# ScalarE issues the first loads of W, SyncE those of x, beta and the bias: a blocked matrix product with a fast multiplication scheme

## The chip, the cores and the metric

The kernel runs on one core of a Trainium2 chip. Times are device microseconds of one execution. PE is TensorE's matmul, PEld its weight load, DVE is VectorE, ACT is ScalarE, POOL is GpSimd, SP is SyncE, and SPq the instructions with which SyncE hands a transfer to the DMA engines. "L377" is line 377 of the kernel.

## The reference

```
B, N, H, L = (2048, 512, 1024, 8)          # rows of x, inner, outputs, factors
s = jnp.einsum('bn,hln->bhl', x, beta)
ssq = jnp.einsum('bn,hln->bhl', x * x, beta * beta)
fm = 0.5 * jnp.sum(s * s - ssq, axis=-1)
linear_out = x @ W.T + b
return fm + linear_out
```

Everything is float32: x is 2048 x 512, beta 1024 x 8 x 512, W 1024 x 512.

## The kernel before

All three parts are products of x (2048 x 512) with a right operand of 512 rows. They are done in passes over the right operand, each with 1024 columns: pass 0 multiplies by W, passes 1 to 8 by an eighth of beta each (the products are then squared and summed over the 8 factors), and a last pass multiplies the squares of x by the summed squares of beta. Within a pass the kernel goes over 8 pairs of row tiles of x (256 rows). A "group" `g` is one pair in one pass, 80 in all.

Each group is a 2 x 2 block product. The blocks of x are A11, A12, A21, A22 and those of the right operand B11, B12, B21, B22. From the third group on a scheme with seven products in place of eight is used, which needs sums of blocks (S1 to S4, T1 to T4). The first two groups (`DIRECT = 2`) use the blocks as they are, since their sums aren't there yet. Every float32 operand is split into a high part that the array takes exactly (`*_hi`, a cast) and the rest (`*_lo`, a subtraction), and each product is three matmuls of 128x128 by 128x512: high x high, high x low, low x high. The casts of the opening are ScalarE's (one is VectorE's), the subtractions VectorE's. For B12 of W alone the high part stands in a slot of `t_lo` (`t_lo[:, 1, T2]`) and the low part in the one beside it.

The order on each engine is written out by hand, and engines meet through semaphores. In the opening TensorE does this:
- nine warm-up matmuls on constants (L461), which wait for no load;
- `first_parts` (L486 to L503), 24 matmuls: x of pair 0, then of pair 1, times B11. It has two halves of the inner dimension (k = 0, 1). For pair 0 each half comes with its half of B11 in one load, `first_p[k]` (tile `first`, which lies in `cs`);
- the products of both pairs with B12 (L509 to L513), 24 matmuls, which appear as L468, L472 and L474 on `t_lo`;
- the products with B21 and B22 (L515 to L520), and then the groups of seven products.

ScalarE waits for `first_p[0]`, then `first_p[1]`, x of pair 1 (L674, L675), B12 (L676, L677), the rest of x of pairs 0 and 1 (L679), B21 and B22, and casts each as it comes. Nothing else is ahead of its first wait but the load of its function table. VectorE follows with the low parts.

All loads are issued by SyncE, in the order of its code:

```
sp.dma_start(first[:, k, 0:2 * P + COLS], first_p[k])      # L377, k = 0 and 1
sp.dma_start(... x_p[1][:, 0:2 * KP * P])                  # L378, x of pair 1
load_first(B12, b12_loaded)                                # L278
sp.dma_start(... x_p[0:DIRECT, :, 2 * KP * P:] ...)        # L381, the rest of x of pairs 0 and 1
sp.wait_ge(first_loaded[KP - 1], 16)
load_first(B21, b21_loaded); load_first(B22, b22_loaded)   # L278
```

and then x of pairs 2 and 3 (L287), the first beta blocks (L282, L283) and the bias (L390). SyncE next waits for TensorE's first products. The loads have these sizes: `first_p` 2 x 384 KB with rows of 3 KB, x of pair 1 256 KB with rows of 2 KB, each block of W 512 KB with rows of 4 KB, the rest of x of pairs 0 and 1 512 KB.

Of the kernel before, what the change touches and what calls it, by code (L numbers as in the profile page):

```python
# [12 lines left out]
KP = 2  # L13
# [13 lines left out]
T1, B22, B11, B21, T2, T3, T4 = range(OPS)  # L27
B12 = T1
# [89 lines left out]
def fm_layer(nc, first_p, x_p, beta_p, w_p, bias, out):  # L118
# [12 lines left out]
    with ExitStack() as ctx:  # L131
# [3 lines left out]
        def sem(name):  # L135
            return ctx.enter_context(nc.semaphore(name))


        with ExitStack() as early:
            def early_sb(name, shape):  # L140
                return early.enter_context(nc.sbuf_tensor(name, shape, f32))

            t_hi_in = early_sb("t_hi_in", [P, 2, OPS, KP, COLS])
# [22 lines left out]
        first_loaded = [sem(f"first_loaded{k}") for k in range(KP)]  # L166
# [3 lines left out]
        b21_loaded = sem("b21_loaded")  # L170
        b12_loaded = sem("b12_loaded")
        b22_loaded = sem("b22_loaded")
# [80 lines left out]
        def t_at(n, op):  # L253

            return t_hi_in[:, 1, op, :, :] if n == 0 else t_lo_in[:, n % 2, op, :, :]
# [17 lines left out]

        @block.sync
        def _(sp):
            def load_first(op, loaded):

                sp.dma_start(t_hi_in[:, 1, op, :, :], w_p[op]).then_inc(loaded, 16)  # L278

            def load_blocks(n):  # L280
                source = q_kept.rearrange("p a b k h -> p (a b) k h") if n == Q_PASS else beta_p[n - 1]
                sp.dma_start(t_lo_in[:, n % 2, 0:2, :, :], source[:, 0:2, :, :]).then_inc(right_loaded, 16)  # L282
                sp.dma_start(t_lo_in[:, n % 2, 2:4, :, :], source[:, 2:4, :, :]).then_inc(left_loaded, 16)  # L283

            def load_x(g):
                blocks = x_at(g)[:, 0:4, :].rearrange("p b c -> p (b c)")
                sp.dma_start(blocks, x_p[pair_of(g)]).then_inc(x_loaded[slot_of(g)], 16)  # L287
# [88 lines left out]
            for k in range(KP):  # L376
                sp.dma_start(first[:, k, 0:2 * P + COLS], first_p[k]).then_inc(first_loaded[k], 16)  # L377
            sp.dma_start(s_lo_in[:, 1, 0:2, :].rearrange("p b c -> p (b c)"), x_p[1][:, 0:2 * KP * P]  # L378
                         ).then_inc(x_second_loaded, 16)
            load_first(B12, b12_loaded)  # L380
            sp.dma_start(s_lo_in[:, 0:DIRECT, 2:4, :].rearrange("p g b c -> p g (b c)"),  # L381
                         x_p[0:DIRECT, :, 2 * KP * P:].rearrange("g p c -> p g c")).then_inc(x_rest_loaded, 16)

            sp.wait_ge(first_loaded[KP - 1], 16)
            load_first(B21, b21_loaded)
            load_first(B22, b22_loaded)
            load_x(2)
            load_x(3)
            load_blocks(1)
# [175 lines left out]
        def _(act):  # L565
# [53 lines left out]
            def split_first_x(k):  # L619
                nc.scalar.copy(s_hi[:, 0, 0:2, k * P:(k + 1) * P], first_x(k)).then_inc(s_hi_ready, 1)  # L620
# [40 lines left out]
            def square_rest(g):  # L661
# [4 lines left out]
                nc.scalar.activation(squares_at(g)[:, COLS:], squares_at(g)[:, COLS:], ACT.Square  # L666
                                     ).then_inc(squared, 1)

            act.wait_ge(first_loaded[0], 16)
            split_first_x(0)  # L670
            act.wait_ge(first_loaded[1], 16)
# [430 lines left out]
```

## Time and profile before

| what | value |
|---|---|
| median of three runs | 775.32 us (775.0 to 775.35) |
| the profiled execution | 775.58 us |
| its span | 773.6 us |
| PE busy | 769.4 us of the span |
| DVE, ACT, POOL busy | 575.0, 395.3, 328.3 us |
| first warm-up matmul, first real matmul | 0.78 us, 4.39 us |

The span runs from the first instruction that the profile shows to the last. Busy times count instructions that compute, so an engine that waits or hands out a transfer isn't busy. A bracket behind a row of the timeline says how long the engine sat idle ahead of it and what ended that.

### The profile page before, as it was taken

The numbers are of one execution on the slowest core, as the hardware profiler recorded it, in microseconds if no ns is written. First come the engines' busy times: TensorE is split into PE (matmuls) and PEld (weight loads), VectorE is DVE, ScalarE is ACT, GpSimd is POOL, SyncE is SP. The second block draws the span as 40 slices with busy tenths as digits, with TensorE's granted clock in tenths as the row PEclk, the third lists the DMA queues.
The fourth block names the chain that finished last, engine by engine and source line by source line (L and its number), as shares of the span: only waits on it lengthen the run. The fifth ranks groups of instructions, "written<-read, shape, count | busy, mean of one in ns | idle before, by whom it ended". The sixth has DMA issues, their size and how long they took to land.

```text
span 773.6 us, 9628 instructions
## 1 busy us (share of the span) xinstructions
PE 769.4 (99%) x3381; PEld 633.5 (82%) x3381; DVE 575.0 (74%) x595; ACT 395.3 (51%) x503; POOL 328.3 (42%) x252
## 2 busy tenths in 40 slices
PE   9999999999999999999999999999999999999998
PEld 6888888888888888888888888888888888888886
DVE  6999289958765876587658765876587658788986
ACT  4674356645554555455545554555455545553430
POOL 0243274345434643454345434543454357334111
PEclk9999999999999999999999999999999999999999
DMA  8697853286604660466046604650565056629843
GB/s 339 262 363 320 311 192 116 79 287 214 222 28 150 217 218 28 149 218 218 28 150 221 221 28 155 218 212 28 169 226 197 28 186 206 224 75 387 337 163 123
DMA packets 64288, 145.34 MB, mean 188 GB/s; under 512 B 4848, under 2 KB 41712, under 8 KB 61936
## 3 DMA queue, kind: packets, MB, share of 16 engines
q1 hardware_dynamic: 64240, 144.72, 52.4%
q8 instruction: 27, 0.44, 0.2%
q14 instruction: 21, 0.17, 0.1%
HBM read 102.76 MB, written 41.94 MB: 187 GB/s over the span
## 4 chain that ended last, share of the span: by engine, by line
PE 98%; DMA 1%; ACT 0%; DVE 0%; SPq 0%; issue 0%
PE bank L472 33%; PE bank L474 33%; PE bank L468 33%; DMA t_hi_in<-w_p 1%; DVE t_lo L889 0%; ACT t_lo L677 0%; SPq L377 0%; ACT cs L725 0%; SPq L378 0%
## 5 line engine op out<-in xcount | busy, mean ns | idle before, releaser
L472 PE MATMUL bank<-t_lo,s_hi 128*128 128x512 f32 x1116 | 434.2, 389 | 0.2 <-DVE t_lo L889 0.2
L468 PE MATMUL bank<-t_hi,s_hi 128*128 128x512 f32 x1108 | 431.1, 389 | 0.0
L474 PE MATMUL bank<-t_hi,s_lo 128*128 128x512 f32 x1108 | 431.0, 389 | 0.0
L472 PEld LDWEIGHTS bank<-t_lo,s_hi 128*128 128x128 f32 x1116 | 209.5, 188 | 44.0 <-DVE t_lo L889 0.6
L468 PEld LDWEIGHTS bank<-t_hi,s_hi 128*128 128x128 f32 x1108 | 208.0, 188 | 43.4 <-ACT r L650 0.3
L474 PEld LDWEIGHTS bank<-t_hi,s_lo 128*128 128x128 f32 x1108 | 208.0, 188 | 43.2
L863 DVE TENSOR_REDUCE sums<-cs 128x256 f32<-128x2048 f32 x64 | 146.3, 2285 | 120.8 <-issue 86.4
L1035 POOL TENSOR_TENSOR r<-r 128x512 f32<-128x512 f32 x70 | 94.8, 1355 | 257.5 <-ACT r L650 257.5
L1039 POOL TENSOR_TENSOR cs<-r 128x512 f32<-128x512 f32 x70 | 94.0, 1343 | 121.6 <-issue 119.9
L658 ACT ACTIVATE cs<-bank 128x512 f32<-128x512 f32 x64 | 38.3, 598 | 204.4 <-PE bank L474 204.4
L731 DVE TENSOR_TENSOR t_lo<-t_lo_in,t_hi 128x1024 fp32r<-128x1024 f32 x63 | 108.2, 1721 | 0.0
L666 ACT ACTIVATE cs<-cs 128x1536 f32<-128x1536 f32 x64 | 95.5, 1493 | 0.0
L1008 POOL TENSOR_TENSOR t_lo_in<-t_lo_in 128x1024 f32<-128x1024 f32 x32 | 78.9, 2465 | 0.1
L854 DVE TENSOR_TENSOR cs<-bank,r 128x512 f32<-128x512 f32 x70 | 48.3, 690 | 33.8 <-PE bank L474 33.8
L567 ACT CAST t_hi<-t_lo_in 128x1024 fp32r<-128x1024 f32 x63 | 65.6, 1046 | 4.0 <-DVE t_lo_in L746 4.0
L644 ACT COPY r<-bank 128x512 f32<-128x512 f32 x71 | 41.8, 588 | 49.5 <-PE bank L474 47.2
L638 ACT COPY r<-bank 128x512 f32<-128x512 f32 x78 | 46.1, 591 | 34.6 <-PE bank L474 34.6
L842 DVE TENSOR_TENSOR r<-bank,r 128x512 f32<-128x512 f32 x78 | 53.4, 684 | 10.5 <-PE bank L474 10.2
L617 ACT CAST s_hi<-s_lo_in 128x1792 fp32r<-128x1792 f32 x16 | 27.2, 1701 | 56.4 <-DVE s_lo_in L812 56.3
L848 DVE TENSOR_TENSOR cs<-bank,r 128x512 f32<-128x512 f32 x70 | 48.4, 691 | 7.6 <-PE bank L474 1.8
L1046 POOL TENSOR_TENSOR acc<-acc,bias_all 128x256 f32<-128x256 f32 x64 | 49.0, 766 | 4.2 <-DMA acc<-acc_kept 4.2
L650 ACT COPY r<-bank 128x512 f32<-128x512 f32 x71 | 41.0, 578 | 2.8 <-PE bank L474 2.8
(77 smaller groups left out, 304.2 us busy)
## 6 DMA issues: line engine op xcount, KB each, us to landing
s_hi<-s_hi_kept SPq DMA_DIRECT2D x30, 896.0 KB, 5.1
s_lo<-s_lo_kept SPq DMA_DIRECT2D x30, 896.0 KB, 7.1
t_lo_in<-beta_p SPq DMA_DIRECT2D x16, 1024.0 KB, 7.1
s_lo_in<-x_p SPq DMA_DIRECT2D x17, 512.0 KB, 6.3
acc_kept<-cs SPq DMA_DIRECT2D x16, 512.0 KB, 5.0
acc<-acc_kept SPq DMA_DIRECT2D x64, 128.0 KB, 5.4
acc_kept<-acc SPq DMA_DIRECT2D x64, 128.0 KB, 1.8
s_hi_kept<-s_hi SPq DMA_DIRECT2D x8, 896.0 KB, 6.3
```

Source lines behind the costliest of these rows:

```text
L468: nc.tensor.matmul(to, s_hi[:, slot, s_op, cols], hi[:, k, :], start=start, stop=False, skip_group_check=True)
L472: nc.tensor.matmul(to, s_hi[:, slot, s_op, cols], lo[:, k, :], start=False, stop=False, skip_group_check=True)
L474: return nc.tensor.matmul(to, s_lo[:, slot, s_op, cols], hi[:, k, :], start=False, stop=stop, skip_group_check=True)
L567: nc.scalar.copy(t_hi[:, n % 2, op, :, :], t_at(n, op)).then_inc(t_hi_ready, 1)
L666: nc.scalar.activation(squares_at(g)[:, COLS:], squares_at(g)[:, COLS:], ACT.Square).then_inc(squared, 1)
L731: nc.vector.tensor_tensor(t_lo[:, n % 2, op, :, :], t_at(n, op), as_f32(t_hi[:, n % 2, op, :, :]), ALU.subtract).then_inc(t_lo_ready, 1)
L842: nc.vector.tensor_tensor(r2[:, :], bank(g, BANK_B), r1[:, :], ALU.add).then_inc(r2_added, 1)
L863: nc.vector.tensor_reduce(sums[:, :, :].rearrange("p r h -> p (r h)"), squares_at(g).rearrange("p (h l) -> p h l", l=L), AX_X, ALU.add).th ...
L1008: nc.gpsimd.tensor_tensor(t_at(n, op), t_at(n, left), t_at(n, right), ALU.subtract).then_inc(t_summed, 1)
L1035: nc.gpsimd.tensor_tensor(r5[:, :], r5[:, :], r7[:, :], ALU.add).then_inc(r57_added, 1)
L1039: nc.gpsimd.tensor_tensor(cs[:, g % 2, 1, 1, :], r5[:, :], r2[:, :], ALU.add).then_inc(c22_added, 1)
L1046: nc.gpsimd.tensor_tensor(acc[:, g % 2, :, :], acc[:, g % 2, :, :], part, ALU.add).then_inc(acc_biased, 1)
```

## The change

ScalarE hands out the three loads of W ahead of its first wait, and SyncE no longer does. SyncE's wait for the second piece of `first_p` goes with them. SyncE's other loads keep their order, the destination and size of every load are the same, and so are all semaphores that ScalarE and VectorE wait for.

```diff
--- before.py
+++ after.py
@@ -273,10 +273,6 @@
 
         @block.sync
         def _(sp):
-            def load_first(op, loaded):
-
-                sp.dma_start(t_hi_in[:, 1, op, :, :], w_p[op]).then_inc(loaded, 16)
-
             def load_blocks(n):
                 source = q_kept.rearrange("p a b k h -> p (a b) k h") if n == Q_PASS else beta_p[n - 1]
                 sp.dma_start(t_lo_in[:, n % 2, 0:2, :, :], source[:, 0:2, :, :]).then_inc(right_loaded, 16)
@@ -377,13 +373,8 @@
                 sp.dma_start(first[:, k, 0:2 * P + COLS], first_p[k]).then_inc(first_loaded[k], 16)
             sp.dma_start(s_lo_in[:, 1, 0:2, :].rearrange("p b c -> p (b c)"), x_p[1][:, 0:2 * KP * P]
                          ).then_inc(x_second_loaded, 16)
-            load_first(B12, b12_loaded)
             sp.dma_start(s_lo_in[:, 0:DIRECT, 2:4, :].rearrange("p g b c -> p g (b c)"),
                          x_p[0:DIRECT, :, 2 * KP * P:].rearrange("g p c -> p g c")).then_inc(x_rest_loaded, 16)
-
-            sp.wait_ge(first_loaded[KP - 1], 16)
-            load_first(B21, b21_loaded)
-            load_first(B22, b22_loaded)
             load_x(2)
             load_x(3)
             load_blocks(1)
@@ -666,6 +657,13 @@
                 nc.scalar.activation(squares_at(g)[:, COLS:], squares_at(g)[:, COLS:], ACT.Square
                                      ).then_inc(squared, 1)
 
+            def load_w(op, loaded):
+
+                nc.scalar.dma_start(t_at(0, op), w_p[op]).then_inc(loaded, 16)
+
+            load_w(B12, b12_loaded)
+            load_w(B21, b21_loaded)
+            load_w(B22, b22_loaded)
             act.wait_ge(first_loaded[0], 16)
             split_first_x(0)
             act.wait_ge(first_loaded[1], 16)
```

On SyncE, the beginning of its program; the names are destination<-source, `cs` holds `first`, `t_hi_in` the blocks of W. Before:

```order
L377 DMA cs<-first_p 128x768 x2
L378 DMA s_lo_in<-x_p 128x512
L278 DMA t_hi_in<-w_p 128x1024
L381 DMA s_lo_in<-x_p 128x2x512
L278 DMA t_hi_in<-w_p 128x1024 x2
L287 DMA s_lo_in<-x_p 128x1024 x2
```

On SyncE now:

```order
L373 DMA cs<-first_p 128x768 x2
L374 DMA s_lo_in<-x_p 128x512
L376 DMA s_lo_in<-x_p 128x2x512
L283 DMA s_lo_in<-x_p 128x1024 x2
L278 DMA t_lo_in<-beta_p 128x2048
```

The three loads of W are gone, and the loads of x and beta follow each other.

On ScalarE, the beginning of its program, before:

```order
L620 ACT_TABLE_LOAD
L620 CAST s_hi<-cs 128x2x128 x2
L673 CAST t_hi<-cs 128x512
L675 CAST s_hi<-s_lo_in 128x512
L677 CAST t_lo<-t_hi_in 128x1024
```

On ScalarE now:

```order
L662 DMA t_hi_in<-w_p 128x1024 x3
L611 ACT_TABLE_LOAD
L611 CAST s_hi<-cs 128x2x128 x2
L671 CAST t_hi<-cs 128x512
L673 CAST s_hi<-s_lo_in 128x512
L675 CAST t_lo<-t_hi_in 128x1024
```

The three loads stand ahead of the table load; everything behind them keeps its order.

## Rows read from the trace of the kernel before

**Rows 1.** The page: span, busy time by engine, and the chain that ended last.

```profile
span 773.6 us, 9628 instructions
...
PE 769.4 (99%) x3381; PEld 633.5 (82%) x3381; DVE 575.0 (74%) x595; ACT 395.3 (51%) x503; POOL 328.3 (42%) x252
...
PE 98%; DMA 1%; ACT 0%; DVE 0%; SPq 0%; issue 0%
```

**Rows 2.** The stretch after the opening: start:end, length, each engine's busy us.

```profile
24.00:770.00 746.00, 746.00 (x3292) 617.48 (x3291) 558.21 (x575) 380.84 (x486) 328.06 (x248) 1.00 0.52 185
```

**Rows 3.** End of the chain: start us, us, what.

```profile
770.32 0.24 PE bank L474
```

**Rows 4.** Timeline from 0 to 20 us: start, us, engine, line, operation, count, [idle before].

```profile
0.73 1.28 ACT L620 ACT_TABLE_LOAD   x1 [0.73 <-PEq L1095]
0.74 0.86 SPq L377 DMA_DIRECT2D cs<-first_p  x2
...
0.78 3.82 PE L461 MATMUL bank<-const-bfloat16-1.0 128*128 128x512 bf16 x9 [0.78 <-PEq L1095]
...
2.12 0.43 SPq L278 DMA_DIRECT2D t_hi_in<-w_p  x1
...
3.81 0.41 ACT L620 CAST s_hi<-cs 128x256 fp32r<-128x256 f32 x1 [1.80 <-DMA cs<-first_p]
...
4.39 0.69 PE L494 MATMUL bank<-t_hi,s_hi 128*128 128x512 f32 x2
...
4.79 0.41 ACT L620 CAST s_hi<-cs 128x256 fp32r<-128x256 f32 x1 [0.57 <-DMA cs<-first_p]
...
5.86 1.52 SPq L287 DMA_DIRECT2D s_lo_in<-x_p  x2
5.91 0.67 PE L494 MATMUL bank<-t_hi,s_hi 128*128 128x512 f32 x2
...
7.08 0.62 ACT L675 CAST s_hi<-s_lo_in 128x512 fp32r<-128x512 f32 x1 [1.35 <-DMA s_lo_in<-x_p]
...
7.75 0.73 PE L494 MATMUL bank<-t_hi,s_hi 128*128 128x512 f32 x2 [0.26 <-ACT s_hi L675]
...
9.06 1.05 ACT L677 CAST t_lo<-t_hi_in 128x1024 fp32r<-128x1024 f32 x1 [1.36 <-DMA t_hi_in<-w_p]
...
10.14 1.22 DVE L889 TENSOR_TENSOR t_lo<-t_hi_in,t_lo 128x1024 fp32r<-128x1024 f32 x1 [1.72 <-ACT t_lo L677]
...
10.88 0.39 PE L468 MATMUL bank<-t_lo,s_hi 128*128 128x512 f32 x1
...
11.42 0.50 PE L472 MATMUL bank<-t_lo,s_hi 128*128 128x512 f32 x1 [0.15 <-DVE t_lo L889]
...
11.99 0.39 PE L468 MATMUL bank<-t_lo,s_hi 128*128 128x512 f32 x1
...
16.54 0.39 PE L474 MATMUL bank<-t_lo,s_lo 128*128 128x512 f32 x1
...
19.82 0.42 DVE L805 TENSOR_TENSOR s_lo_in<-s_lo_in 128x256 f32<-128x256 f32 x1
```

**Rows 5.** The first load of `first_p` alone: its issue, and its time to landing.

```profile
L377 SPq DMA_DIRECT2D cs<-first_p x1: 388/388/388, 0.7 to 0.7; - x1
...
DMA to landing us min/median/max: 3.1/3.1/3.1
```

**Rows 6.** Stretches of the opening; last columns: PEclk, DMA share, GB/s.

```profile
0.00:3.00 3.00, 2.23 (x6) 0.86 (x7) 0.00 (x0) 1.28 (x1) 0.20 (x4) 1.00 0.41 119
3.00:4.00 1.00, 1.00 (x4) 0.31 (x3) 0.18 (x1) 0.18 (x1) 0.00 (x0) 1.00 1.05 397
5.00:6.00 1.00, 1.00 (x6) 0.57 (x5) 0.90 (x3) 0.72 (x2) 0.00 (x0) 1.00 0.37 92
8.00:9.00 1.00, 1.00 (x4) 0.53 (x4) 0.42 (x1) 0.00 (x0) 0.00 (x0) 1.00 1.07 422
```

**Rows 7.** The page's DMA queues: packets, MB, share.

```profile
q1 hardware_dynamic: 64240, 144.72, 52.4%
```

## The prediction

> **What bounds the kernel now.** I read the page first: PE is busy 769.4 of a span of 773.6 us, and the chain that ended last is 98% PE [rows 1]. The reader is to see that nothing but PE's start, its holes and its end can move the time. Then the stretches: from 24 to 770 us PE has no hole at all, 746.00 busy of 746.00 us [rows 2], and its last matmul begins at 770.32 [rows 3]. What is left is the opening, read from the timeline of the first 17 us [rows 4].
>
> The reader is to see there how thin the opening's slack is. The nine warm-up matmuls on constants take 3.82 us from 0.78, to 4.60. The first piece of `first_p` lands 3.1 us after its issue at 0.74 [rows 5], and ScalarE's first cast starts at 3.81. The first real matmul follows at 4.39, when the warm-up is all but over. Matmuls that wait for nothing go at one every (16.54 - 11.99) / 20 = 0.2275 us. The 24 matmuls of `first_parts` run from 4.39 to 10.88, that is 6.49 us where 24 x 0.2275 = 5.46 would do: 1.03 us lost, partly before the second half of `first_p` is cast and most of it at 7.75, behind x of pair 1. The first product with B12 waits again: its second matmul starts at 11.42, where 10.88 + 0.23 = 11.11 was due, 0.31 us for `t_lo` of B12. So all that earlier loads could give back in the whole kernel is 1.03 + 0.31 = 1.34 us, and the B12 product, had its first matmul been followed without a gap, in effect starts at 11.19.
>
> The profiled execution took 775.58 us, 0.26 over the median of 775.32; the sums below are differences, added to 775.58 and then lowered by 0.26. 0.2% of this kernel is 1.55 us: about what its measurement can tell from no change. All of the 1.34 us is less than that.
>
> **The change, part by part.**
>
> *ScalarE issues three loads ahead of its first work.* No row shows ScalarE issuing a load. SyncE's issues take 0.43 us each at the start, and 1.52 / 2 = 0.76 with a long queue [rows 4]. Three of them put the table load, which starts at 0.73 now, at 2.02 (with 0.43) or 3.01 (with 0.76), and its 1.28 us end at 3.30 or 4.29. I take 0.43, as an empty queue is what SyncE has at that time too: 3.30 is before the cast at 3.81, so this costs nothing; the load of `first_p` hides it. The other end, 4.29, would delay the first cast by 0.48 us if `first_p` still landed at 3.81, and nothing if it lands as late as I expect below.
> The Trainium skill (ScalarE: Activation LUTs, "What ACT_TABLE_LOAD costs" and the table-load gate before it) puts a table load at about 2.7 us; by that it would end at an estimated 4.7. This case's row has 1.28 us, and the row decides.
>
> *SyncE no longer issues B12, B21, B22 and has no wait.* It loses one issue of 0.43 ahead of the rest of x for pairs 0 and 1, and its wait for the second piece of `first_p`, which landed at 4.79. So x of pairs 2 and 3, beta and the bias are issued some 3.3 us earlier (x of pair 2 at about 2.6 for 5.86). All of them stand behind the rest of x in SyncE's own order, none is wanted before 19 us (the first use of x of pair 2 is the sum at 19.82 [rows 4]), and they can't pass what PE waits for in the opening. Gain and cost on the path: nothing.
>
> *W's 1.57 MB now compete with `first_p`.* This is the term that decides. Before, one queue served loads in the order of their issue: `first_p` (2 x 0.393 MB), x of pair 1 (0.262 MB), and B12 only then. Now B12, B21 and B22 are offered at the same time as `first_p`, from another queue. No row shows two queues of loads side by side: the page has one, q1 [rows 7], beside two for instructions. So the cost is bounded. From below: W gets only what `first_p` leaves, and costs nothing. From above: each of the two queues gets a turn, row by row, and W's rows are 4 KB against 3 KB of `first_p` and 2 KB of x of pair 1. Between them lie equal shares by bytes. In the rows of a stretch each [rows 6] the DMA engines move 119 GB/s over the first three us and 397 in the fourth, so 0.356 MB by 3.0 and 0.753 MB by 4.0, and I let it go on at 400 (422 is seen between 8 and 9). The engines' share is already 1.05 in 3 to 4 us: nothing is free there for a second queue, what it gets is taken.
>
> Now 0.393 MB are moved by 3.1 and land at 3.81, so landing comes 0.7 us after the bytes. Shares by bytes: the first piece needs 0.786 MB, moved at 4.1, landed at 4.8; the second 1.57 MB, 6.05, landed 6.75; x of pair 1 2.10 MB, 7.4, landed 8.1. Shares by rows: 0.918 MB, landed 5.1; 1.835 MB, landed 7.4; 2.62 MB (with which W is through), landed 9.4.
> PE follows. From the first landing it is 4.39 - 3.81 = 0.58 to the first matmul, from the second 5.91 - 4.79 = 1.12, from that of x of pair 1 7.75 - 7.08 = 0.67 [rows 4].
> - By bytes: first matmul 5.4, its six end 6.75; the next six wait for 6.75 + 1.12 = 7.87 and end 9.23; x of pair 1 is ready at 8.77; twelve more end at 9.23 + 2.73 = 11.96. Against 11.19: **+0.77 us**.
> - By rows: 5.7, then 7.4 + 1.12 = 8.52, ending 9.89; x of pair 1 ready at 10.07; twelve more end at 12.80. Against 11.19: **+1.6 us**.
> I take the middle, +1.2 us, as the row length does differ but nothing shows that turns go by rows.
>
> The Trainium skill speaks against the change too (DMA: Bandwidth & Descriptors, "Queues, rings and completion order", and "Issuing engines are not separate DMA queues"): loads of ScalarE and SyncE run on the same 16 DMA engines, which take turns between the queues by packet, and a second issuer only saves issue time. Its turns would give the sum between the two above; the trace of before, with one queue, can't confirm it.
>
> *B12 comes earlier.* In either reckoning B12 lands before x of pair 1, so ScalarE's cast of it (1.05 us, right behind the 0.62 us one of x of pair 1) and VectorE's 1.22 us no longer end after PE wants them: by rows 9.4 + 0.62 + 1.05 + 1.22 = 12.3, with PE there at 12.8. The 0.31 us wait and the 0.26 us hole at 7.5 go; both are inside the sums already, since PE is charged from landings. What is late next is the second piece of `first_p`.
>
> *Sum:* issues 0, SyncE 0, sharing and PE's new waits +1.2: 775.58 + 1.2 = 776.8 profiled, less 0.26 is **776.5**.
>
> **The rivals.**
> - *W does not hold up `first_p`; the waits go (other side).* Place: the landing at 3.81. Should W's rows start behind `first_p` by a us or so, or should the slow stretch at 5 to 6 us (92 GB/s, share 0.37 [rows 6]), when B12 was issued and yet little moved, be filled by the other queue, PE would start at 4.39 as now and lose less than 1.34 us. For it: that trough, over 1 us of engines all but idle with loads queued. Against: the share of 1.05 at 3 to 4. It decides if the first piece lands before about 4.2. Time: 775.32 - 1.34 = 774.0 at best, 774.9 with a third of it. Chance 0.20. A page of the Trainium skill (Perfetto Trace Analysis, its list on DMA) has the same hope: balancing over issuers may help where descriptor generation bounds. The trough could be that; nothing here shows it.
> - *PE falls back to its low clock.* Warm-up matmuls go at 3.82 / 9 = 0.42 us each, 512 columns at 1.2 GHz, later ones at 0.2275, as they only can at 2.4. The page's granted clock is 1.00 in all stretches, so it is the spacing that tells. PE would now stand from 4.60 to 5.4 or 5.7, and again for 1.1 to 1.5 us before the second piece; no hole of before is longer than 0.3. If one more stretch like the warm-up ran at the low level, nine matmuls at 0.42 for 0.23 cost 1.8 us more: 776.5 + 1.8 = 778.3. Decides if the first real matmuls are some 0.43 apart. Chance 0.10, with slow first rows of W (a queue's first packets blocking both) in the same figure.
> - *The forecast's own case,* shares of either kind: 0.70, its own range 775.7 to 777.3.
>
> **How the numbers follow.** 776.5 is the likeliest case. The range reaches down to 774.8, into the first rival, and up to 778.0, short of the second: it leaves out perhaps 0.07 below and 0.09 above. Slower by over 1.55 us (above 776.87): all of the clock rival, 0.10, and a third of the forecast's case (shares by rows, +1.6, is just there), 0.25: 0.35. Faster by over 1.55 us needs more than the waits hold; 0.02 for what I don't see. Within: 0.63.
>
> **What would show it.** The first cast of ScalarE at 4.8 to 5.1 for 3.81; the second cast of x of pair 0 at 6.7 to 7.4 for 4.79; first real matmul at 5.4 to 5.7; the three W loads landed before 9.5, B22 above all; the wait on VectorE's `t_lo` at the first B12 product gone; no hole in PE after 13 us; GB/s near 400 already at 3 to 6 us. It is wrong if `first_p` lands by 4.2 (then W does not compete, and the time is at or below 775.3), if it lands after 6 (W gets more than its turn), if matmuls behind the first wait are 0.43 apart, or if PE shows a hole later, which I excluded.

## The result

Median 777.63 us (777.51 to 778.08, 7 runs) against 775.32 us (774.88 to 775.38, 7 runs): the ratio is 1.0032, 95% interval 1.0023 to 1.0042. The change costs 2.3 us. The range, 774.8 to 778.0, holds the time; the forecast of 776.5 named the way but half of the size.

The page of the changed kernel, its span, busy times and chain:

```profile
span 775.7 us, 9628 instructions
...
PE 769.2 (99%) x3381; PEld 633.6 (82%) x3381; DVE 574.7 (74%) x595; ACT 395.6 (51%) x503; POOL 328.7 (42%) x252
...
PE 98%; DMA 1%; ACT 0%; SPq 0%; issue 0%
```

PE's work is the same (769.2 us for 769.4), and the span is 2.1 us longer. In the chain beside PE stands a load of `first_p` now, where the kernel before had the load of B12. From 24 to 770 us nothing changed, and the last matmul is late by 772.38 - 770.32 = 2.06 us [rows 3]:

```profile
24.00:770.00 746.00, 746.00 (x3292) 617.48 (x3292) 557.48 (x575) 382.17 (x487) 327.79 (x248) 1.00 0.52 184
```

```profile
772.38 0.24 PE bank L465
```

So the loss is in the opening, whose timeline (all engines) reads:

```profile
0.73 1.38 ACTq L662 DMA_DIRECT2D t_hi_in<-w_p  x3
...
0.77 3.62 PE L452 MATMUL bank<-const-bfloat16-1.0 128*128 128x512 bf16 x9 [0.77 <-PEq L1093]
...
2.14 1.28 ACT L611 ACT_TABLE_LOAD   x1 [2.14 <-issue]
...
5.55 0.41 ACT L611 CAST s_hi<-cs 128x256 fp32r<-128x256 f32 x1 [2.13 <-DMA cs<-first_p]
...
6.12 0.70 PE L485 MATMUL bank<-t_hi,s_hi 128*128 128x512 f32 x2 [1.73 <-DVE t_hi L878]
...
7.65 0.40 ACT L611 CAST s_hi<-cs 128x256 fp32r<-128x256 f32 x1 [1.70 <-DMA cs<-first_p]
...
8.72 0.70 PE L485 MATMUL bank<-t_hi,s_hi 128*128 128x512 f32 x2 [0.92 <-ACT t_hi L671]
...
9.62 0.62 ACT L673 CAST s_hi<-s_lo_in 128x512 fp32r<-128x512 f32 x1 [1.04 <-DMA s_lo_in<-x_p]
...
10.29 0.73 PE L485 MATMUL bank<-t_hi,s_hi 128*128 128x512 f32 x2
...
11.02 0.73 PE L489 MATMUL bank<-t_hi,s_lo 128*128 128x512 f32 x2
11.22 1.22 DVE L887 TENSOR_TENSOR t_lo<-t_hi_in,t_lo 128x1024 fp32r<-128x1024 f32 x1 [0.26 <-ACT t_lo L675]
...
13.40 0.39 PE L459 MATMUL bank<-t_lo,s_hi 128*128 128x512 f32 x1
...
13.63 0.39 PE L463 MATMUL bank<-t_lo,s_hi 128*128 128x512 f32 x1
```

Against [rows 4]: the first cast at 5.55 for 3.81, the second at 7.65 for 4.79, that of x of pair 1 at 9.62 for 7.08. PE is idle from 4.39 to 6.12 and from some 7.8 to 8.72. The B12 product starts at 13.40 and runs on without a gap. The prediction puts its start before at 11.19 in effect, from its second matmul. But the third was late too: the fourth began at 11.99 [rows 4], so the start was in effect at 11.99 - 3 x 0.2275 = 11.31. The loss is 13.40 - 11.31 = 2.09 us, which agrees with the 2.06 of the last matmul. ScalarE's table load ends at 3.42, long before the first piece lands.

Three stretches of [rows 6] again (last columns: PEclk, DMA share, GB/s), and what each queue moved from 3 to 5 us; q10 is ScalarE's, q1 SyncE's. The columns are packets, MB and share of the DMA engines; a packet is a row here, but for a few of 4 bytes that end a load:

```profile
0.00:3.00 3.00, 2.23 (x6) 0.87 (x7) 0.00 (x0) 0.86 (x1) 0.20 (x4) 1.00 0.40 67
3.00:4.00 1.00, 1.00 (x4) 0.30 (x3) 0.00 (x0) 0.42 (x1) 0.00 (x0) 1.00 0.96 335
5.00:6.00 1.00, 0.00 (x0) 0.00 (x0) 0.44 (x2) 0.41 (x1) 0.00 (x0) 1.00 1.01 408
```

```profile
q10 hardware_dynamic: 111, 0.42, 58.7%
q1 hardware_dynamic: 113, 0.32, 40.2%
```

In this stretch the queues take turns row by row: 111 of W against 113 of `first_p`, and so 0.42 MB against 0.32. The start is slower too, 67 GB/s over three us for 119, while the trough at 5 to 6 us is gone (408 GB/s for 92).

### The profile page after: what moved, and what is told of

Same layout as the page of the kernel before. It is cut to its first block, busy times and chain, and to the rows that moved or that the text cites. A ratio compares the mean times of both kernels' runs of the same rounds, so it can differ in the third digit from the quotient of the medians.

```text
span 775.7 us, 9628 instructions
## 1 busy us (share of the span) xinstructions
PE 769.2 (99%) x3381; PEld 633.6 (82%) x3381; DVE 574.7 (74%) x595; ACT 395.6 (51%) x503; POOL 328.7 (42%) x252
## 4 chain that ended last, share of the span: by engine, by line
PE 98%; DMA 1%; ACT 0%; SPq 0%; issue 0%
PE bank L459 33%; PE bank L465 33%; PE bank L463 33%; DMA cs<-first_p 1%; PE bank L485 0%; PE bank L489 0%; PE bank L493 0%; ACT cs L723 0%; ACT t_hi L671 0%; ACT s_hi L611 0%; SPq L373 0%
```

## The experiments

My theory after the result: two queues take turns, so W's bytes hold up `first_p`, and the whole loss is that. Its rivals: SyncE's missing wait crowds the opening; ScalarE's issues and its late table load cost; W is dear from ScalarE wherever it is issued; PE's clock falls in its idle time. Times are medians of 11 runs where not said otherwise, beside runs of the kernel before on the same chip (775.40 us for the first four, 775.23 for the next, 775.24 for the last), and the ratios with their 95% intervals. Every "spare" load goes to memory that nothing uses until 19.8 us. Each kernel has one profiled execution. Those of tiny_first (776.02 us), tiny_b12 (775.41), act_late (783.04) and touch_late_b12 (776.35) are the slowest runs of their kernels, so their rows tell less of the medians.

| run | us | ratio |
|---|---|---|
| hold_off | 775.41 | 1.0000 (0.9991 to 1.0008) |
| act_b12 | 776.15 | 1.0016 (1.0007 to 1.0025) |
| spare_4k (6 runs) | 777.83 | 1.0030 (1.0019 to 1.0042) |
| spare_tiny | 774.93 | 0.9991 (0.9982 to 1.0000) |
| spare_1k | 777.04 | 1.0022 (1.0013 to 1.0031) |
| tiny_first | 775.31 | 0.9999 (0.9990 to 1.0008) |
| tiny_b12 | 775.07 | 0.9997 (0.9988 to 1.0006) |
| act_late (4 runs) | 782.00 | 1.0089 (1.0075 to 1.0103) |
| touch_late | 775.07 | 0.9997 (0.9988 to 1.0006) |
| touch_late_b12 | 775.11 | 0.9998 (0.9989 to 1.0007) |
| act_b12_warm | 776.08 | 1.0011 (1.0002 to 1.0020) |
| touch_sp | 776.20 | 1.0011 (1.0002 to 1.0020) |

**hold_off: the SyncE part alone.**

```diff
-            sp.wait_ge(first_loaded[KP - 1], 16)
             load_first(B21, b21_loaded)
```

> The kernel before without SyncE's wait for the second piece of first_p; SyncE still issues all loads, W's in their old places. Theory of the queues (two queues take turns, so W's bytes delay first_p): nothing competes here, first cast at 3.8 us, second cast at 4.8, time 775.3, within 0.3. Theory of SyncE (the loads of x 2 and 3, beta and the bias, no longer held back, are what crowds the opening): the whole loss of 2.3 us is here, 777.6, with the first cast at 5.5.

No change in the time; first cast at 3.81, second at 5.01 (4.8 was expected). SyncE's earlier loads aren't the loss.

**act_b12: a third of the bytes.**

```diff
-            load_first(B12, b12_loaded)          # SyncE
+            nc.scalar.dma_start(t_at(0, B12), w_p[B12]).then_inc(b12_loaded, 16)   # ahead of ScalarE's first wait
```

> ScalarE issues B12 alone ahead of its first wait, 0.52 MB in place of 1.57; SyncE issues B21 and B22 where it did, behind its wait. Theory of the queues: the first piece of first_p still lands near 5.5 us, since both queues are full that long, but the second comes 0.52 MB / 400 GB/s = 1.3 us earlier than in the changed kernel, at 6.3 for 7.65; PE then runs through from the first landing and loses 0.4 us on before: 775.7. Theory of the order of W (it is B21 and B22 that hurt): first_p back at 3.8 and 4.8, and B12's wait gone, 775.0. Theory of a fixed price for a second queue: as the changed kernel, 777.6.

Timeline of ScalarE and PE:

```profile
5.29 0.41 ACT L619 CAST s_hi<-cs 128x256 fp32r<-128x256 f32 x1 [2.84 <-DMA cs<-first_p]
...
5.87 0.70 PE L493 MATMUL bank<-t_hi,s_hi 128*128 128x512 f32 x2 [1.10 <-DVE t_hi L880]
...
6.41 0.41 ACT L619 CAST s_hi<-cs 128x256 fp32r<-128x256 f32 x1 [0.72 <-DMA cs<-first_p]
...
11.67 0.39 PE L467 MATMUL bank<-t_lo,s_hi 128*128 128x512 f32 x1
```

The second piece is cast at 6.41, where 6.3 was expected; the first is as late as with three loads (5.29). The B12 product starts at 11.67, +0.36 us on 11.31, and the profiled execution is 0.35 us longer than that of before. The median, 775.40 + 0.75, is above the 775.7 that was expected, for the 11 runs fell into two groups, six from 775.93 to 776.15 and five from 777.31 to 777.71; the profile is of the lower (775.93), which is what the theory foresaw. act_b12_warm below takes that up.

**spare_4k: the bytes alone.** SyncE's program is the one before, every load of W in its old place.

```diff
+            for i, op in enumerate((B12, B21, B22)):      # ScalarE, ahead of its first wait
+                nc.scalar.dma_start(spare[i], w_p[op].rearrange("p k c -> p (k c)")).then_inc(spare_loaded[i], 16)
```

> The kernel before, with SyncE as it was, and three more loads of 0.52 MB by ScalarE ahead of its first wait, with rows of 4 KB (the same three blocks of W) to memory that is still unused. Theory of the queues: first_p lands as in the changed kernel, first cast 5.55, second 7.65; B12 comes through SyncE after 3.1 MB at about 10.7, its low part at about 13.0, just in time for PE at 13.4: 777.6. Theory that it was taking W from SyncE's order that cost: 775.3, first cast at 3.8.

```profile
5.46 0.40 ACT L621 CAST s_hi<-cs 128x256 fp32r<-128x256 f32 x1 [2.04 <-DMA cs<-first_p]
7.57 0.40 ACT L621 CAST s_hi<-cs 128x256 fp32r<-128x256 f32 x1 [1.71 <-DMA cs<-first_p]
```

The whole loss is back, with both casts within 0.1 us of the changed kernel's, although W came through SyncE as before. It is the competing bytes, not who issues the W that is used.

**spare_tiny: the issues without the bytes.**

```diff
+                nc.scalar.dma_start(spare[i][:, 0:16], w_p[op][:, 0, 0:16]).then_inc(spare_loaded[i], 16)
```

> As before, with three loads by ScalarE ahead of its first wait that move 64 bytes in each of 128 rows of B12, B21 and B22 to unused memory: the issues and the late table load, without the bytes. Theory of the queues: first cast at 3.8 to 3.9, time within 0.3 of 775.3. Theory of the issues (ScalarE's three issues and the table load behind them are the loss): first cast late by 1 us or more, 776.5 or above. A third possibility: the slow stretch of DMA at 5 to 6 us is the first touch of W by every DMA engine; touched early, B12 lands before 8.7 for 9.0 and the 0.31 us wait goes: 775.0.

ScalarE's timeline, PE's, and the stretch from 5 to 6 us:

```profile
2.14 1.28 ACT L621 ACT_TABLE_LOAD   x1 [2.14 <-issue]
...
4.12 0.41 ACT L621 CAST s_hi<-cs 128x256 fp32r<-128x256 f32 x1 [0.69 <-DMA cs<-first_p]
...
4.69 1.19 PE L495 MATMUL bank<-t_hi,s_hi 128*128 128x512 f32 x2
...
5.68 0.96 PE L499 MATMUL bank<-t_hi,s_lo 128*128 128x512 f32 x2
...
6.32 0.62 ACT L680 CAST s_hi<-s_lo_in 128x512 fp32r<-128x512 f32 x1
...
6.94 0.61 PE L495 MATMUL bank<-t_hi,s_hi 128*128 128x512 f32 x2
...
8.32 1.05 ACT L682 CAST t_lo<-t_hi_in 128x1024 fp32r<-128x1024 f32 x1 [1.37 <-DMA t_hi_in<-w_p]
```

```profile
2.00:3.00 1.00, 1.00 (x4) 0.43 (x3) 0.00 (x0) 0.86 (x1) 0.00 (x0) 1.00 0.57 190
5.00:6.00 1.00, 1.00 (x3) 0.81 (x3) 0.76 (x2) 0.62 (x2) 0.00 (x0) 1.00 0.97 315
```

Three issues and the table load at 2.14 cost nothing: the first cast waited for its load, not for the table. The signs of the third possibility came: 315 GB/s in the trough for 92, x of pair 1 cast at 6.32 for 7.08, B12 at 8.32 for 9.06. The price is the first piece, 4.12 for 3.81, since the third us is slower (190 GB/s). By its median this is the fastest kernel here, 0.47 us under before, with an interval that ends at 1.0000.

**spare_1k: turns by rows, or shares by bytes.** As spare_4k, to memory in rows of 1 KB (the end of the line is left out):

```diff
+                nc.scalar.dma_start(s_lo_in[:, 0:4, S1 + i, :], w_p[op].rearrange("p k (r c) -> p (k r) c", c=256)
```

> As spare_4k, the same 1.57 MB of W a second time ahead of ScalarE's first wait, but to memory in rows of 1 KB. If the two queues take turns row by row, first_p with its 3 KB rows gets 3/4 of the rate for 3/7: second cast at 5.9 to 6.2 for 7.57 in spare_4k, PE at the end of first_parts at 11.2 for 13.3, time 775.4. If they share by bytes, the second cast stays near 7.2 to 7.6 and the time at 777 or above.

The second cast came at 6.26 us for 7.57, next to the 5.9 to 6.2 of turns by rows. The time didn't follow (777.04): B12 was cast only at 10.28, and PE, at the B12 product by 12.08, waited for its low part. The queues from 3 to 5 us:

```profile
q10 hardware_dynamic: 347, 0.36, 52.2%
q1 hardware_dynamic: 138, 0.37, 47.8%
```

Bytes are about even here, 0.36 against 0.37 MB, and rows aren't: 347 to 138. So this run is against strict turns by rows as well. ScalarE's issues with split rows also took 2.13 us for 1.38, and its queue moved nothing before 3 us, which let the first piece go ahead: VectorE casts from it at 3.96. ScalarE's cast is at 4.19, for here its table load ran from 2.90 to 4.18, the one trace in which it was in the way, by some 0.2 us. The run is inconclusive on the rule; it shows only that short rows hold `first_p` up less.

**tiny_first and tiny_b12: which touch fills the trough.** The same small loads, from `first_p` (the end of the line is left out), and from B12 alone:

```diff
+                nc.scalar.dma_start(spare[i][:, 0:16], first_p[i % 2][:, 256 * (i // 2):256 * (i // 2) + 16]
---
+            nc.scalar.dma_start(spare[0][:, 0:16], w_p[B12][:, 0, 0:16]).then_inc(spare_loaded[0], 16)
```

> As spare_tiny, but the three loads of 64 bytes a row read first_p in place of B12, B21 and B22. If the trough of DMA at 5 to 6 us is the first touch of W, it is back: under 150 GB/s there for 315 in spare_tiny, x of pair 1 cast at 7.1 for 6.3, B12 at 9.1 for 8.3. If a second queue or the small loads as such filled it, it stays filled and B12 is cast by 8.4.

> One load of 64 bytes a row of B12 alone by ScalarE ahead of its first wait. If the first touch of the block that comes next makes the trough, B12 is cast by 8.4 as in spare_tiny, while first_p is delayed by less than the 0.3 us there (first cast 3.9); time 774.9 or a little less. If the three blocks of W must each be touched, B12 is early and the rest of W as before, same time. If it does nothing, 775.3.

The stretch from 5 to 6 us, first of tiny_first, then of tiny_b12:

```profile
5.00:6.00 1.00, 1.00 (x6) 0.57 (x4) 0.91 (x3) 0.93 (x2) 0.00 (x0) 1.00 0.78 189
```

```profile
5.00:6.00 1.00, 1.00 (x3) 0.81 (x3) 0.96 (x3) 0.92 (x3) 0.00 (x0) 1.00 0.90 311
```

With `first_p` read in place of W the stretch is at 189 GB/s and x of pair 1 is cast at 7.76; with B12 touched it is at 311 and x of pair 1 is cast at 5.99, B12 at 7.80. The sign set for W's first read, under 150 GB/s in tiny_first, did not come: 189 lies between the 92 of before and 311. The rows of B12 themselves, each a record of the trace, say more. Of its first rows four took 1.3 to 1.6 us each before, where later rows take 0.16, and five took 1.6 to 2.0 in hold_off; in tiny_first ten took some 0.5; in tiny_b12 none of the first twenty was above 0.41. So slow first reads of B12 are shown, and one small load of it mostly takes them away. Why a touch of `first_p` halves them too stays open.

The time hardly follows: 0.16 us under before, within its interval. The reason is in PE's rows of tiny_b12:

```profile
4.73 1.19 PE L495 MATMUL bank<-t_hi,s_hi 128*128 128x512 f32 x2
5.73 1.04 PE L499 MATMUL bank<-t_hi,s_lo 128*128 128x512 f32 x2
...
7.07 0.62 PE L495 MATMUL bank<-t_hi,s_hi 128*128 128x512 f32 x2
```

PE waits for no load behind 4.73 here. But its first six real matmuls take 7.07 - 4.73 = 2.34 us where 6 x 0.2275 = 1.37 would do: they are up to 0.5 us apart, PE's clock was still at the lower of its two levels. (The column PEclk shows 1.00 there as well; the spacing tells.) Before, waits and gaps cost 11.31 - 4.39 - 5.46 = 1.46 us; here the later start costs 4.73 - 4.39 = 0.34 and the clock 0.97, together 1.31, and the B12 product starts at 11.18 for 11.31. spare_tiny has the same, 6.94 - 4.69 = 2.25 us for six. No run here has both, loads that are early and a clock that is up by the first real matmul, so what that would be worth is not shown.

**act_late: W from ScalarE, behind `first_p`.** In the changed kernel the three `load_w` lines move behind ScalarE's third cast.

> The changed kernel with ScalarE's three loads moved behind its third cast (the high part of B11's second half), so that they are issued at 5.7 to 7.1 us, behind first_p. Theory of the queues: first_p is back at 3.8 and 4.8, x of pair 1 lands earlier than before (6.3 to 7.1), but W now shares with x of pairs 2 and 3: B12's low part ready at 11.8 to 12.2 for 11.4, time 775.9 to 776.8, between the two kernels. Theory that W from ScalarE's queue is dear wherever it is issued: 777.6.

A miss by 5 us. `first_p` is indeed back (casts at 3.95 and 4.87), but W doesn't come. Queues from 5 to 8.5 us, then from 12.5 to 16; PE; and the stretch from 16 to 20 us:

```profile
q1 hardware_dynamic: 469, 1.18, 96.2%
```

```profile
q1 hardware_dynamic: 135, 0.97, 66.1%
q10 hardware_dynamic: 137, 0.50, 35.0%
```

```profile
14.77 0.50 PE L459 MATMUL bank<-t_lo,s_hi 128*128 128x512 f32 x1 [3.78 <-ACT t_lo L675]
16.03 0.80 PE L463 MATMUL bank<-t_lo,s_hi 128*128 128x512 f32 x1 [0.76 <-DVE t_lo L887]
...
18.32 0.63 PE L459 MATMUL bank<-t_lo,s_hi 128*128 128x512 f32 x1
18.75 0.63 PE L463 MATMUL bank<-t_lo,s_hi 128*128 128x512 f32 x1
...
22.15 0.39 PE L459 MATMUL bank<-t_lo,s_hi 128*128 128x512 f32 x1
```

```profile
16.00:20.00 4.00, 3.97 (x9) 3.17 (x10) 2.33 (x2) 1.05 (x1) 0.00 (x0) 0.50 0.89 360
```

B12 was issued at 4.88, ahead of the third cast (5.18) that it stands behind in the code, and landed 8.8 us later. From 5 to 8.5 us SyncE's queue alone moved loads, 469 packets; the first row of W in the trace is at 8.66. From there W took turns with x of pairs 2 and 3 and with beta, all of them handed out before it: 137 packets against 135 from 12.5 to 16 us, and as beta's rows are 8 KB, half of beta's bytes. So W did not wait for SyncE's whole list, and what held it from 4.88 to 8.66 stays open. PE stood for 3.78 us and again for 0.76, and then its clock was at the lower of its two levels, granted 0.50 from 16 to 20, matmuls 0.43 us apart until 22.15. The price adds up: the product in effect at 16.03 - 0.23 = 15.80 for 11.31 is 4.49; 14 matmuls in 22.15 - 16.03 = 6.12 us for 14 x 0.2275 = 3.19 is 2.93; together 7.42 of the 7.46 by which the profiled execution is longer than before. So place does matter, but the other way: W that joins behind SyncE's list is worse off than beside `first_p`.

**touch_late, touch_late_b12, touch_sp: can the touch be had without its price?**

```diff
+            nc.scalar.copy(r1[:, 0:1], nc.const_aps.tensor(1.0, [P, 1], f32))   # so that the table load comes first
             ... the small loads of spare_tiny, or that of tiny_b12
---
+            sp.dma_start(cs[:, 0, 0, 0, 0:16], w_p[B12][:, 0, 0:16])            # touch_sp: SyncE, behind first_p
```

> The kernel before; ScalarE copies one column of a constant first, so that the table load comes first, and then issues the three loads of 64 bytes a row of B12, B21 and B22, at 2.2 to 3.6 us. If a second queue slows first_p only while its own first reads are slow at the start, and the touch still is ahead of B12's turn, first_p is back near 3.8 and 4.8, the trough at 5 to 6 us is filled, x of pair 1 is cast at 6.3 for 7.1, B12 at 8.3 for 9.1, the B12 product is in effect at 10.7 for 11.2: 774.8. If the touch must come before 2 us, the time is 775.3 with the trough as before.

> As touch_late with the touch of B12 alone, one issue at 2.2 us. The least that should fill the trough: as touch_late, 774.8, or 0.1 to 0.3 less, since ScalarE is free by 2.7 and not by 3.6. If each block of W has its own slow first reads, B21's cast is no earlier than in the kernel before.

> As touch_late_b12, but SyncE issues the small load of B12, in its own queue between first_p and x of pair 1. If what fills the trough is that another queue's loads can pass a queue whose first reads are slow, nothing is won here: x of pair 1 cast at 7.1 or later, since the slow reads now stand ahead of it too, and 775.3 to 775.9. If it is enough that B12 was touched early, x of pair 1 is cast at 6.5 and the time is 774.9.

ScalarE's first rows in touch_late, and its stretch from 5 to 6 us:

```profile
0.73 1.28 ACT L672 ACT_TABLE_LOAD   x1 [0.73 <-PEq L1103]
0.79 0.87 ACTq L674 DMA_DIRECT2D cs<-w_p  x2
...
2.02 0.19 ACT L672 COPY r<-const-float32-1.0 128x1 f32<-128x1 f32 x1
3.90 0.41 ACT L621 CAST s_hi<-cs 128x256 fp32r<-128x256 f32 x1 [1.68 <-DMA cs<-first_p]
```

```profile
5.00:6.00 1.00, 1.00 (x5) 0.82 (x4) 0.90 (x3) 0.83 (x2) 0.00 (x0) 1.00 0.77 220
```

The premise fell: the table load doesn't hold back issues that stand behind it. They went out at 0.79, beside it. So the touch came no later than in spare_tiny, and yet the first cast is at 3.90, the stretch at 220 GB/s, x of pair 1 at 7.09 (6.3 was expected), B12 at 8.40. With one trace of each, what makes the difference to spare_tiny stays open. All four touches from ScalarE end within 0.2 us of each other (774.93 to 775.11), none apart from before. In the slowest of the 11 runs of touch_late_b12, the profiled one, B12 was touched as well and yet x of pair 1 is cast at 8.30 and B12 at 9.56: a touch doesn't make the loads early each time. From SyncE's own queue the touch loses: x of pair 1 is cast at 8.09 and the median is 776.20, 0.3 above the range expected for that case. That slow first reads ahead of x of pair 1 in the same queue hold it up, and that another queue's can be passed, fits this and isn't shown further.

**act_b12_warm: the two groups of act_b12.**

```diff
-WARM_UP = 9
+WARM_UP = 12
```

> act_b12 with 12 warm-up matmuls in place of 9. The runs of act_b12 fell into two groups, 775.9 to 776.2 and 777.3 to 777.7, 1.4 us apart. Theory of the clock: the upper group are runs in which PE's idle time after the warm-up left it at 1.2 GHz for the first matmuls; with PE busy until its first real matmul at 5.9 us the upper group is gone or rare, median 775.9 to 776.1. If the two groups come from the landings of first_p, they stay, at the same distance.

All 11 runs lie between 775.69 and 776.47; the upper group, five runs of 11 before, is gone. But the expectation's condition didn't hold: the twelve ended at 4.97, and PE was idle for 1.26 us before its first real matmul at 6.23, longer than in the trace of act_b12 (1.10 us, from 4.77 to 5.87). What differs is the rise of the clock. In the trace's record of it, it comes at 3.71 us here, ahead of the three added matmuls, and at 5.10 in act_b12, when PE had already gone idle. An upper run in which it came still later would fit; no trace of one exists, and the two sets were taken on different chips. So the clock as the cause of the groups is argued and not shown.

## Why the prediction was right in its way and short in its size

- **What bounds it.** Right. All of the loss is in PE's opening.
- **Issues and table load cost nothing.** Right: ScalarE's three issues took 1.38 us (0.46 each for 0.43), the table load ended at 3.42 for 3.30, and spare_tiny, which has both, is not slower.
- **SyncE's part costs nothing.** Right, hold_off.
- **Sharing, +0.77 to +1.6, taken as +1.2.** The mechanism was right: spare_4k alone gives the loss, act_b12 with a third of the bytes gives a smaller one, and in the changed kernel rows of both queues go one for one. The step that was mis-sized is "I take the middle": the rows' end, +1.6, was the one to take, 0.4 us. Landings foreseen by rows were 5.1, 7.4 and 9.4; the casts came at 5.55, 7.65 and 9.62.
- **The start.** I carried 119 GB/s over the first three us across from the kernel before. It became 67, and PE began each of its three stretches late on the rows' reckoning: 6.12 for 5.7, 8.72 for 8.52, 10.29 for 10.07. The last counts, 0.22. The third us is slow wherever W is touched or loaded at the start (157 GB/s in the changed kernel, 190 in spare_tiny, 196 in tiny_b12, for 304 before), less so with `first_p` touched (253). So W's first reads beside those of `first_p` are the likely cause, not a shown one.
- **PE behind the last landing.** I gave its twelve matmuls 12 x 0.2275 = 2.73 us from 10.07. They took 13.40 - 10.29 = 3.11, for the second pair waits for VectorE's low part (at 11.02, 0.73 behind). The kernel before had the same 0.4 (7.75 to 10.88 is 3.13 us), and I had read it only as slack.
- **The start of the B12 product before.** 11.19 was read too early by 0.12 us; it was 11.31. The waits before were thus 1.46 us and not 1.34, and by rows the sum gives +1.5.
- **The sum.** 1.2 + 0.4 for the rows + 0.22 for the start + 0.38 for VectorE's low part - 0.12 = 2.08, for the 2.09 of the traces. That the medians are 2.3 apart and the profiled executions 2.05 comes from the 0.26 that the one of before was above its median; the changed kernel's was at its median, so lowering the forecast by 0.26 made it too low as well. That the range held the time owes something to its width.
- **The rival on the other side** (W doesn't hold up `first_p`) is wrong for loads of W's size. Its argument was half right: the trough was there to be filled, and a touch fills it in part or whole, without a gain in time beyond the intervals.
- **The rival of the clock.** In the profiled execution of the changed kernel it didn't happen: after 1.7 us of idle time matmuls at 6.12 and 6.66 are 0.27 apart, not 0.43. In act_late, after 3.78 us, it did, at 2.9 us. And in spare_tiny and tiny_b12 the clock wasn't up yet, for 0.9 to 1.0 us.

The Trainium skill (DMA: Bandwidth & Descriptors, "Queues, rings and completion order") has the DMA engines take turns between queues packet by packet, several descriptors in each as a rule. For long rows the traces show even turns, 111 to 113 for W and `first_p`, 137 to 135 for W and beta; I had put that rule between my two sums, and the rows' end would have been its place. No row here shows how many rows one turn has, and 347 rows of 1 KB to 138 in spare_1k are not turns of one row each. The same page of the Trainium skill, "Issuing engines are not separate DMA queues", has all loads run on the same DMA engines and interleave; spare_4k agrees. The 2.7 us of the Trainium skill (ScalarE: Activation LUTs, "What ACT_TABLE_LOAD costs") are a sum there, of 1.28 us for the load and 1.38 us for a drain. The rows here agree with the first, 1.28 us before and after; of the second they show nothing, for in touch_late the load ends at 2.01 and the copy behind it starts at 2.02. The prediction had not read this split.

## What to carry to other kernels

A second issuing engine gives the loads no more bandwidth where one queue fills the DMA engines already (397 GB/s before and 335 after in the fourth us), but it changes their order: what it issues at the start goes one for one with the load that the whole kernel waits for. Before moving a load to another queue, ask which load it will share with, and count rows as well as bytes; and a load issued late from the second queue can stand still for microseconds and then has to share. When DMA stands nearly still with loads queued, look for the first read of a new tensor; one small load of it, from the other queue, brought its cast forward here in three traces of four. Then look whether PE can use it: here its clock was not yet up, and no such load won time beyond its interval.

## What the runs showed of the hardware

- The first rows of a block of W are slow to read: four of 1.3 to 1.6 us before, where 0.16 is usual, and a us at 92 GB/s. One load of 8 KB of that block, issued 4 us ahead from another queue, lifts the us to 311 in tiny_b12.
- Issues that stand behind ScalarE's table load go out beside it, at 0.79 us with the load at 0.73.
- A queue that joined at 4.88 us moved its first row at 8.66, while the other went on (act_late).
- PE's clock rises at a different time from trace to trace, though the nine warm-up matmuls are the same: in hold_off they take 3.39 us, so that it rose within them, and in spare_tiny, after 4.00 us of them, the first six real matmuls still took 2.25 us, until 6.94.
